# A one-core block of two expert layers around a gated scan: idle sums behind indirect transfers, a new order of stages, time-contiguous tiles, another buffer for the normalised rows

## The reference

```
x = x + 0.5 * ffn(layernorm(x))
x = x + attn(layernorm(x))
x = x + 0.5 * ffn(layernorm(x))

ffn(x):   16 experts, top 2 of a softmax over x @ Wr + br, weights made to sum to 1
          h = gelu(x @ W1[e] + b1[e]);  o = h @ W2[e] + b2[e]     128 -> 256 -> 128
          y = x + sum over the two experts of weight * o
attn(x):  xn = rmsnorm(x) * gamma; q, k, v, g = xn @ wq, wk, wv, wg;  a = xn @ wa (complex)
          a -> sigmoid(|a|) * exp(i * angle(a))
          y_t = a_t * y_(t-1) + k_t * v_t   along the 256 tokens;  (q * Re(y) * silu(g)) @ wo
```

## Time and profile before

| | |
|---|---|
| time of a run, median of 3 | 880.05 us (880.0 to 881.23) |
| profiled execution, first to last instruction | 994.3 us |
| beside its span, no other time of that execution is given; span less median | 114.2 us |
| granted TensorE clock, mean | 0.858 |
| busy: PE, DVE, ACT, POOL | 725.1, 546.3, 514.7, 590.6 us |
| moved by DMA | 167.13 MB, 168 GB/s |

### The profile page before, as it was taken

One profiled execution on the slowest core, in us unless ns is written; L12 is line 12 of the kernel. 1 busy time (PEld: TensorE's weight loads), 2 busy tenths in 40 slices (PEclk: granted clock), 3 DMA queues, 4 the chain that ended last, 5 costly groups with the idle time before them and its releaser, 6 DMA issues.

```text
span 994.3 us, 15862 instructions
## 1 busy us (share of the span) xinstructions
PE 725.1 (73%) x4409; PEld 607.2 (61%) x4410; DVE 546.3 (55%) x1352; ACT 514.7 (52%) x1071; POOL 590.6 (59%) x551
## 2 busy tenths in 40 slices
PE   4775888786876888669777967685968648977761
PEld 4234788685366873469644867534958627777650
DVE  7983103106689955799745996647876455010201
ACT  1111556455777637676277773576664315444340
POOL 2277441555777747758467457378657545655555
PEclk9995899889977989789788779795989759999986
DMA  9995587774146833176441456321758517778863
GB/s 327 299 348 165 149 234 228 208 202 130 40 123 195 224 111 105 42 202 194 121 124 46 129 161 202 99 66 40 217 167 250 141 41 199 221 207 226 234 201 103
DMA packets 188846, 167.13 MB, mean 168 GB/s; under 512 B 18976, under 2 KB 176480, under 8 KB 187744
## 3 DMA queue, kind: packets, MB, share of 16 engines
q1 hardware_dynamic: 120736, 106.83, 36.6%
q0 software_dynamic: 16384, 33.72, 11.5%
q10 hardware_dynamic: 51648, 25.63, 8.8%
HBM read 104.57 MB, written 61.51 MB: 167 GB/s over the span
## 4 chain that ended last, share of the span: by engine, by line
PE 48%; issue 12%; ACT 12%; another core or an unknown queue 9%; SPq 7%; DVE 5%; DMA 5%; ACTq 0%; DVEq 0%
PE bank L786 17%; PE bank L803 16%; PE bank L863 7%; DMA WUP<-up_weights 4%; PE bank L776 4%; ACT eo L540 2%; SPq L319 2%; PE bank L758 2%; SPq L360 1%; SPq L330 1%; ACT hidT L532 1%; PE bank L702 1%; ACT ci L623 1%; ACT xsT L551 1%
## 5 line engine op out<-in xcount | busy, mean ns | idle before, releaser
L487 POOL DMA_INDIRECT got<-rows_out,IDX x256 | 285.8, 1117 | 194.2 <-ACT eo L540 86.5
L786 PE MATMUL bank<-xsT,WUP 128*128 128x128 f32 x1564 | 240.0, 303 | 77.4 <-ACT xsT L551 51.1
L786 PEld LDWEIGHTS bank<-xsT,WUP 128*128 128x128 f32 x1564 | 218.8, 216 | 85.9 <-issue 75.2
L803 PE MATMUL bank<-W,hidT 128*128 x1564 | 221.0, 286 | 41.5 <-ACT hidT L532 32.1
L803 PEld LDWEIGHTS bank<-W,hidT 128*128 128x128 f32 x1564 | 199.3, 199 | 51.4 <-issue 49.6
L466 POOL DMA_INDIRECT rows_in<-XL,IDX x128 | 157.1, 1227 | 109.3 <-DVE IDX L1039 46.5
L474 POOL DMA_INDIRECT rows_in<-XL,IDX x128 | 136.3, 1065 | 91.7 <-ACT eo L540 53.7
L540 ACT ACTIVATE eo<-bank,xs 128x128 f32<-128x128 f32 x391 | 122.7, 367 | 109.9 <-PE bank L803 74.6
L532 ACT ACTIVATE hidT<-bank 128x512 f32<-128x512 f32 x200 | 118.1, 591 | 116.1 <-PE bank L786 72.8
L551 ACT ACTIVATE xsT<-bank 128x256 f32<-128x256 f32 x200 | 74.0, 377 | 86.2 <-remote 39.2
L863 PE MATMUL bank<-XT,WA 128*128 128x512 f32 x192 | 94.6, 654 | 21.2 <-DVE qg L1090 10.4
(11 more groups left out here) (150 smaller groups left out, 900.4 us busy)
## 6 DMA issues: line engine op xcount, KB each, us to landing
WUP<-up_weights SPq DMA_DIRECT2D x400, 128.0 KB
xs<-rows_in SPq DMA_DIRECT2D x100, 258.0 KB
rows_out<-eo ACTq DMA_DIRECT2D x91, 256.0 KB
rows_in<-kv SPq DMA_DIRECT2D x16, 774.0 KB, 12.1
X<-in_L_attn_x SPq DMA_DIRECT2D x4, 1024.0 KB, 7.7
rows_in<-XL,IDX POOLq DMA_INDIRECT x256
got<-rows_out,IDX POOLq DMA_INDIRECT x256
out<-X SPq DMA_DIRECT2D x4, 1024.0 KB
```

The costliest lines, as they stand in the source:

```text
L487: pool.indirect_dma_start(got[:, k, j, :], None, rows_out[SLOT[f, g, half]][0:rows, :], bass.IndirectOffsetOnAxis(IDX[:, g, j, k:k + 1], 0 ...
L786: ins = pe.matmul(ps[2 + u % 2][:, k * P:(k + 1) * P], WUP[:, u, a, c * P:(c + 1) * P], xsT[:, u % 2, a * P:(a + 1) * P], start=True, stop ...
L803: ins = pe.matmul(o, hidT[:, v, (2 * a + c) * P:(2 * a + c + 1) * P], W2[:, ds(e * H + c * D, D)], start=(c == 0), stop=(c == 1))
```

## The change

Five things change.

1. POOL issues a sum of 96 columns of the identity with themselves into a buffer that nobody reads, behind 289 of the 512 indirect transfers (table APART), and waits for its end before it goes on.
2. PAIRS_BY holds much less: its last entry was 199 and is 72; that of PRODUCTS_BY was 92 and is 29.
3. ORDER: in each expert layer that runs beside an attention (E(0,2), E(0,3), E(1,0)) the pieces 8 to 20 and 20 to 24 become one piece 8 to 24, and A3 comes behind it and is followed by T of the next group. S and N(None, g + 1) come ahead of A3(g). E(0,1) is cut at pair 20, E(1,1) at pairs 4 and 12 in place of 12 alone; R(1,3) goes ahead of the first four pairs of E(1,2), and K(1,2) behind the first four of E(1,1). In group 2 all of C(0,2) goes ahead of K(1,0) and A2(1).
4. XN lies in cr, no longer in kv.
5. Layout: tile l of a group now holds 128 consecutive tokens of one sequence. The load and the store of x therefore move 512-byte pieces; XT is written and kv is read contiguously, where a stride of 16 elements stood before.

```diff
+IDLE = 96
-         ("E", 0, 2, 0, 8, 20), ("G", 1, 0, 0, 4), ("S", 1), ("A3", 0), ("E", 0, 2, 0, 20, 24), ("N", None, 1),
-         ("W", 0, 3), ("B", 0, 2, 1), ("T", 1), ("B0", 0, 3), ("A0", 1), ("N", (1, 0), None), ("A", 1), ("I", 1),
...
+         ("N", None, 1), ("E", 0, 2, 0, 8, 24), ("A3", 0), ("G", 0, 3, 3, 4), ("T", 1), ("W", 0, 3), ("B", 0, 2, 1),
+         ("B0", 0, 3), ("N", (1, 0), None), ("A0", 1), ("A", 1), ("I", 1), ("B", 0, 3, 0), ("H", 1), ("B", 0, 3, 1),
...
-            ("G", 0, 2, 3, 4): (76, 77, 78, 78, 79, 79, 79, 79),
+            ("G", 0, 2, 3, 4): (15, 15, 15, 15, 15, 15, 15, 15),
...
+APART = {
...
+         ("G", 0, 3, 2, 3): (0, 1, 1, 1, 1, 1, 1, 1),
...
-    x_v = x.rearrange("(g b) (c l) d -> g (b c) l d", g=G, l=T)
-    out_v = out.rearrange("(g b) (c l) d -> g (b c) l d", g=G, l=T)
+    x_v = x.rearrange("(g b) (l p) d -> g p (b l) d", g=G, p=P)
+    out_v = out.rearrange("(g b) (l p) d -> g p (b l) d", g=G, p=P)
...
+        idle = sb("idle", [P, IDLE], f32)
...
-        XN = kv[:].rearrange("p (l d) -> p l d", l=T)
+        XN = cr[:].rearrange("p (l d) -> p l d", l=T)
...
+            def keep_apart(st, i):
+                if APART[st][i]:
+                    link(pool.tensor_tensor(idle[:], ident[:, 0:IDLE], ident[:, 0:IDLE], add))
...
                         pool.indirect_dma_start(got[:, k, j, :], None, rows_out[SLOT[f, g, half]][0:rows, :],
                                                 bass.IndirectOffsetOnAxis(IDX[:, g, j, k:k + 1], 0)).then_inc(got_in[j // 4], 16)
+                        keep_apart(("G", f, g, lo, hi), 2 * j - lo * T // 2 + k)
...
-                    act.activation(by_time(XT[:])[:, 4 * i:4 * i + 4, :], ps[i][:].rearrange("p (l c) -> p l c", l=4), ACT.Copy,
-                                   scale=GS[:, 0:1]).then_inc(xnT_sb, 1)
+                    act.activation(XT[:, i * 512:(i + 1) * 512], ps[i][:], ACT.Copy, scale=GS[:, 0:1]).then_inc(xnT_sb, 1)
...
-                        ins = pe.matmul(ps[4 + i][:, j * D:(j + 1) * D], by_time(kv[:])[:, 4 * i + j, :], WO[:],
+                        ins = pe.matmul(ps[4 + i][:, j * D:(j + 1) * D], kv[:, (4 * i + j) * P:(4 * i + j + 1) * P], WO[:],
...
+                    else:
+                        dve.wait_ge(y_ready, ga)
```

More of the change, by code:

```diff
@@ L36 @@
 ROUND = 12582912.0
-ORDER = [("N", (0, 0), None), ("N", (0, 1), None), ("R", 0, 0), ("L", 0, 1), ("P", 0, 0, 0), ("P", 0, 1, 0),
[26 rows of a table removed]
+ORDER = [("P", 0, 0, 0), ("P", 0, 1, 0), ("N", (0, 0), None), ("N", (0, 1), None), ("R", 0, 0), ("L", 0, 1),
[25 rows of a table added]
 HALVED = ((1, 3),)
@@ L239, in build @@
         tmp = [S[:, i * W:(i + 1) * W] for i in range(4)]
-        XN = kv[:].rearrange("p (l d) -> p l d", l=T)
-        def by_time(buf):
-            return buf.rearrange("p (c l) -> p l c", l=T)
+        XN = cr[:].rearrange("p (l d) -> p l d", l=T)
         zeros = kv[:]
@@ L467, in scatter @@
                                                 XL[:, b, j, :], None).then_inc(first_put[i], 16)
+                        keep_apart(("P", f, g, half), j - first)
                 for i, part in enumerate(parts):
@@ L475, in scatter @@
                                                 XL[:, b, j, :], None).then_inc(scattered[which], 16)
+                        keep_apart(("P", f, g, half), tiles + j - first)
             def gather(n, f, g, lo, hi):
```

## The result

The changed kernel takes 957.57 us (956.17 to 958.58, 4 runs), the kernel before 880.02 us (878.49 to 881.23, 4 runs) beside it. The ratio is 1.0875 [1.0852, 1.0898]: 77.6 us slower, where 28 us less were forecast. A ratio here leaves out runs over 1.5% above the fastest of their kernel, so it can differ a little from the quotient of two medians.

The account below looks back on a forecast made before the run. It took a line of stages on PE, with gaps waiting for ACT or DVE, as the bound. 42.8 us saved less 15 given back is 27.8: 880.05 becomes 852 (own range 842 to 864, wider 826 to 900), chance 43%.

Parts of the forecast that it names:

- The step that failed: Whole kernel: profile pauses make most of the 114.2 us between span and median, so a forecast difference holds in both.
- under the sums: POOL: 289 sums cost 90 us, 45 in spare time early; POOL ends at 894 against a span of 966, free.
- The size of a sum: POOL: a sum of 96 columns takes 0.31 us, between 0.25 in proportion and 0.38 on a line.
- The rival's point of decision: POOL behind the first gather: sums dearer than 0.16 us take its work past 689 us and make it decide.
- The rival that came true: POOL's chain from the first gather on becomes the bound and the kernel slower: 889 to 935, about 895 us; chance 26%.
- Layout: PE's line: contiguous output product operand saves 12 us, contiguous XT copies 6.4; 512-byte pieces of x cost nothing.
- One piece of E: Three group boundaries: one pipeline filling and drain in place of two saves 4.8 us each, 14.4 in all.
- T behind A3: Three boundaries: ACT's 3.18 us normalisation of XN is covered by PE's output product, saving 9.5 us.
- new cut of E(0,1) at pair 20: With E(1,1)'s at pair 4: two fillings cost 9.6 us, covered PE waits return 10.1, so +0.5 together.
- less 6: DVE's side of moving T: a later quarter of C eats its lead; 2 us charged each, 6 in all.
- The 33 sums of the tail: Last 56 gathers: 33 sums, 10 us, against 32 pairs at 2.0 us; 5 us charged (0 to 10).
- The rival of bursts: Sums spread a scatter's transfers, so slow pairs gain 0.15 us for each of 200, 30 us: 822; chance 10%.

Follow-up runs that it names:

- quiet: Sort of job, named for its traces, with no unknown queue in the chain; the unedited kernel before takes 884.12 us in the first job.
- pausing: Sort of job, named for its traces, where matmuls pause; the unedited kernel before takes 981.0, 996.2, 981.4 and 978.5 us in four such jobs.

## Why the prediction was wrong

**The step that failed** is the last one ahead of the sum: "I take these for most of the 114.2 us between span and median, and a forecast difference as the same in both", and with it, under the sums, "it ends at 894 where it now ends at 987, if nothing holds it. Against a span of 966 that is free". The first half was true: the quiet executions have spans of a run's length and no pauses. The second was not. The pauses of that profile stretch PE's line and leave POOL's work as it is, so they showed POOL room that a run without them does not have. From the first gather on, the windows of the kernel before (pausing) and of the changed kernel without sums (quiet, to its end) say it:

```profile
167.80:987.10 819.30, 609.54 (x3782) 513.85 (x3781) 466.36 (x1041) 460.22 (x942) 515.67 (x462) 0.85 0.53 150
...
153.60:863.40 709.80, 567.92 (x3781) 479.80 (x3780) 468.63 (x1044) 460.70 (x942) 523.27 (x462) 0.89 0.61 175
```

POOL works 516 us in the one and 523 in the other, and is idle for 304 and 187. Less 462 steps of 0.30 us, the room is 165 us where I read it and 48 in a quiet run, 6 of them behind the last gather. I named that weakness and still priced the sums against the long span. Against a run that ends at 850, POOL at 894 is the bound by itself.

**The size of a sum.** Forecast 0.31 us, measured 0.353 beside an idle DVE and 0.500 in the mean. With the right length and the wrong room the sums would still have been called free or nearly; with the right room and 0.31 us the forecast would have been slower. The rival's point of decision, 0.16 us a piece, was nearly right: fills of 0.208 us give 0.7% slower.

**The rival that came true** is the first: POOL becomes the bound. Its place and cause are right. Its 889 to 935 us end 22 us short. Its parts behind the first gather against measured: transfers and steps 650, here 643; sums 76 + 46, here 127.8 + 5.6; a wait for IDX, none forecast, 10.7; three steps of 1.26 us, 3.8; last steps 5, here 6.1. The first gather starts at 159.2, forecast 158. 159 + 643 + 133 + 11 + 4 + 6 = 956 of the 956.4.

**Layout.** Forecast 12 + 6.4 = 18.4 us, measured 15.9. The output product went from 7.26 to 3.84 us, 3.4 saved where 3.0 stood. Four copies of XT in a row take 2.4 us (3.75 before, 2.16 forecast), so they save 1.35 and not 1.6. 4 x 4.8 = 19 us, of which 15.9 reach the run.

**One piece of E, and T behind A3.** Forecast 14.4 + 9.5 us, measured nothing within the interval, together with the new cuts and holds: the kernel with all of these and no sums is 2.5 us slower than the layout alone. The 4.8 us a boundary came from the 12.6 us of the four pairs, which are 8.3 in a quiet trace: much of what I took for a filling was a pause, beside the one of 3.1 us that I had seen and left out, and the drain of 2.26 us is one of 0.72. The two profiled executions show a gain and two losses. The first attention ends on PE at 244.1 us in the kernel without sums and at 237.6 in the layout alone: its products start 3.6 us later, behind the new cut of E(0,1) at pair 20 that I had near nothing, and take 2.9 us longer, as the first of them run at half pace (0.85 us from one to the next, later 0.43), with a granted clock of 0.89 against 1.00, after transposes with gaps between them. From there to the end of the last output product the new order takes 436.8 us (to 680.9) and the old 449.7 (to 687.3), so it gains 12.9, where my sum had some 18 (14.4 + 9.5 less 6). Of the 6.4 us that it then leads by, 3 are lost at the tail. These are single executions, 5.5 us quicker than the median for the kernel without sums, so the parts are not more certain than that.

**A miscount.** The 33 sums of the tail stand in the last 64 gathers; the last 56 have 27. It changes that term by 2 us.

**What held.** ACT's normalisation beside the output product, the price of the new layout's load (none seen) and the steps between two instructions on POOL were as forecast. The rival of bursts, 822 us, was wrong in a quiet job, and half right in a pausing one: transfers that stand apart do speed the pairs up there, through the stops that they prevent.

**What stays open.** Why a job is quiet or pausing, and what stops PE, ACT and the other queues during a train of indirect transfers. The trace shows the stop and that it follows the spacing of the transfers and the job; no row shows the resource. The Trainium skill (DMA: Bandwidth & Descriptors, Queues, rings and completion order) has a rule, told there of transfers that SyncE and ScalarE issue: the semaphore increment is a strongly ordered write that lands only after every earlier write of its DMA engine, on all its queues. No run here shows whether that is the cause. Late increments need not be all of it: in the stopped stretch PE also halts inside a group, with no wait that the profile shows (the eighth matmul of an up product at 117.81 us, 1.74 us after the seventh, put down to issue). Whether every pausing job pauses alike is also open: the kernel before took 978 to 996 in them.

## What to carry to other kernels

Compare the span of a profile with the time of a run before summing anything from it. If they differ by a tenth, every engine that is not on the chain shows room that the run does not have; price the work that an edit adds against the short time. And an instruction that does nothing may be there for a condition that the timing job does not show: here it costs 87 us in one sort of job and saves 276 in the other (18 against the kernel before, which has holds instead), so run such an edit in both before keeping or dropping it.

## What was not expected of the hardware

- The same program on the same kind of chip takes 880 or 980 us, by job. A program with closely spaced indirect transfers takes 871 or 1254.
- In a pausing job, a train of indirect transfers 1.26 us apart stops PE and ACT for up to 24 and 18 us at a time; the DMA engines move 70 GB/s in place of 280, POOL goes on undisturbed. In the same stretch, 1.45 to 1.51 us apart lets half to three quarters of the matmuls through, and at 1.64 nothing stops.
- A GpSimd sum of 96 columns takes 0.352 us by itself and up to 2.44 behind a VectorE operation of two inputs; a fill of the same size 0.192 us.
- A stationary operand read at a stride of 16 elements makes 32 matmuls with their loads take 7.26 us, a contiguous one 3.84; a load alone 0.312 us and 0.192.
